# One layer pair on one core: x's first two tiles loaded singly at the head of ScalarE's queue, A and x transposed and the first u taken in the network's waits, loads of SyncE reordered

## What is computed

```python
# layer 0, on x
h = gelu(cond @ W0 + b0); h = gelu(h @ W1 + b1); att = softmax(h @ W2 + b2)
agg_w = einsum('bk,koi->boi', att, weight); agg_b = att @ bias_k
o = einsum('boi,bih->boh', agg_w, x) + agg_b[:, :, None]
logits = o @ Wr.T                      # 4 experts, the best 2, softmax over them
mid = einsum('tf,erf->ter', o, A)
x = x + sum_e gates * einsum('ter,eor->teo', mid, B) * 4
# layer 1, on the new x
o = conv1d(x, weight, 9 taps, 4 groups) + (cond @ c_weight.T)[:, :, None] + bias
h = relu(layernorm(o @ gw1.T + gb1) * gamma + beta); gates = h @ gw2.T + gb2
# 8 experts, best 2, an expert counts only if it was chosen at most 1536 times
x = x + o @ W.T + lora(o, lora_A, lora_B, w) / 16
```

## Time and profile before

| what | us, or as said |
|---|---|
| median of 3 runs | 302.68 |
| lowest and highest | 301.27, 303.99 |
| profiled execution | 302.07 |
| its span, first to last instruction | 300.3 |
| TensorE busy (matmul) | 288.7 |
| VectorE, ScalarE, GpSimd busy | 195.4, 125.3, 95.1 |
| packets of the queue of SyncE, share of the 16 DMA engines' span | 69.1% |
| HBM rate over the span | 175 GB/s |

### The profile page before, as it was taken

One profiled execution on the slowest core, in us unless ns is written; L12 is line 12 of the kernel. 1 busy time (PEld: TensorE's weight loads), 2 busy tenths in 40 slices (PEclk: granted clock), 3 DMA queues, 4 the chain that ended last, 5 costly groups with the idle time before them and its releaser, 6 DMA issues.

```text
span 300.3 us, 6135 instructions
## 1 busy us (share of the span) xinstructions
PE 288.7 (96%) x1982; PEld 236.5 (79%) x1982; DVE 195.4 (65%) x506; ACT 125.3 (42%) x263; POOL 95.1 (32%) x124
## 2 busy tenths in 40 slices
...
GB/s 142 186 339 143 154 252 233 212 213 75 220 185 210 87 218 211 178 93 181 228 189 104 161 224 207 104 154 204 129 104 163 187 206 6 0 2 188 320 331 280
DMA packets 74400, 52.75 MB, mean 176 GB/s; under 512 B 44405, under 2 KB 61477, under 8 KB 74377
## 3 DMA queue, kind: packets, MB, share of 16 engines
q1 hardware_dynamic: 72936, 51.37, 69.1%
...
...
HBM read 35.67 MB, written 16.78 MB: 175 GB/s over the span
## 4 chain that ended last, share of the span: by engine, by line
PE 54%; DMA 14%; SPq 12%; DVE 8%; issue 5%; ACT 4%; POOL 1%; DVEq 0%; ACTq 0%
PE ps_g L1139 10%; PE ps_d L1139 9%; DMA xg<-x1d 8%; PE ps_c L1277 7%; DMA x1d<-xq 7%; PE ps_a L1100 5%; PE ps_t L1293 3%; SPq L353 3%; PE ps_a L1089 3%; SPq L356 2%; ACT xq L632 2%; PE ps_d L1318 2%; PE ps_d L1319 2%; PE ps_d L1500 1%; PE ps_d L1505 1%
## 5 line engine op out<-in xcount | busy, mean ns | idle before, releaser
L512 POOL TENSOR_TENSOR o1l<-o,o1h 128x512 fp32r<-128x512 f32 x30 | 39.4, 1313 | 150.2 <-ACT o L644 150.2
L1139 PE MATMUL ps_d<-wt_hi,o1h 128*128 128x336 f32 (+1 forms) x120 | 41.1, 342 | 0.3 <-DVE y_all L961 0.3
L1139 PE MATMUL ps_d<-wt_hi,o1l 128*128 128x336 f32 (+1 forms) x120 | 38.7, 323 | 0.0
L1139 PE MATMUL ps_d<-wt_lo,o1h 128*128 128x336 f32 (+1 forms) x120 | 38.6, 322 | 0.0
L1277 PE MATMUL ps_c<-xg,cw 96*32 96x512 f32 x256 | 34.1, 604 | 3.1 <-DMA xg<-x1d 3.1
L955 DVE TENSOR_TENSOR oT<-ps_c,biasT 128x512 f32<-128x512 f32 x32 | 21.9, 686 | 22.8 <-PE ps_c L1277 21.9
L1139 PE MATMUL ps_g<-wt_hi,o1h 128*128 128x336 f32 x112 | 35.6, 318 | 0.6 <-ACT tmp_all L659 0.4
L1139 PE MATMUL ps_g<-wt_hi,o1l 128*128 128x336 f32 x112 | 35.5, 317 | 0.0
L1139 PE MATMUL ps_g<-wt_lo,o1h 128*128 128x336 f32 x112 | 35.4, 316 | 0.0
L632 ACT ACTIVATE xq<-y_all 128x512 f32 (+1 forms) x29 | 31.9, 1152 | 7.3 <-DMA x1d<-xq 4.1
L1100 PEld LDWEIGHTS ps_a<-pm,xT 128*128 128x128 f32 x256 | 30.2, 192 | 1.4 <-issue 0.8
...
## 6 DMA issues: line engine op xcount, KB each, us to landing
xg<-x1d SPq DMA_DIRECT2D x64, 254.0 KB, 5.1
...
xs<-in_x_dram SPq DMA_DIRECT2D x6, 1024.0 KB, 6.2
...
y_all<-in_x_dram ACTq DMA_DIRECT2D x2, 512.0 KB, 5.2
y_all<-in_x_dram SPq DMA_DIRECT2D x1, 1024.0 KB, 5.7
```

The source lines that it names most:

```text
L512: pool.tensor_tensor(lo, o1[t % 2][:, :, :], hi.bitcast(fp32), ALU.subtract).then_inc(s_o1l, 1)
L1139: last = T.matmul(bank[:, 0:columns], a[:, Q - 1 - q, :], w[:, q, first:first + columns], start=(q == 0 and n == 0), stop=(q == Q - 1 and ...
```

## The change

- **Loads of x[0].** On ScalarE's queue x[0] came as two halves of 512 KB, fourth and sixth. Now its first tile is the second load, its second tile the fourth, and the last two tiles the fifth. b2 and fside move from there to SyncE's queue.
- **SyncE's loads.** A and Wr (aw) are issued ahead of the four loads of the mixing weights; b2 ahead of them, the context weights and fside behind. The load of x[3] leaves the set-up: it is issued in step 1, ahead of gather(1, 1). Layer 1's A is one load of 1024 runs of 256 B, where it was eight of 512 runs of 64 B each, ahead of the taps; ga is stored as blocks of 16 for that, and three instructions read or write it by blocks.
- **TensorE's head.** A is transposed behind t1(0, 0), ahead of W2's product; t1 and the products of u (`u_first`, into ps_d[1]) are placed one tile at a time; the transposes of B move behind the last of them; the context's transpose and product move back; four `keep_busy` of one are dropped, and two of one become two.
- **B.** ScalarE copies the transposed B twice (b_plain, b_hi), VectorE takes b_lo from the copy behind gates0(0). The bias's transpose moves behind t1(1, 1). delta(0, 0) waits for b_lo.
- The ones are set by VectorE first; GpSimd clears the taps later.

```diff
-        ga = sb("ga", [P, Q, GC])
+        ga = sb("ga", [P, GC // R1, Q, R1])
...
             sp.dma_start(w1n, w1).then_inc(s_ld["w1"], 16)
-            sp.dma_start(ctxn, ctxw).then_inc(s_ld["ctx"], 16)
             sp.dma_start(w2n, w2).then_inc(s_ld["w2"], 16)
+            sp.dma_start(b2b, b2.partition_broadcast(P)).then_inc(s_ld["b2"], 16)
+            sp.dma_start(aw[0:ER0], ffa.rearrange("e r h -> (e r) h")).then_inc(s_ld["aw"], 16)
+            sp.dma_start(aw[ER0:UC], ffr).then_inc(s_ld["aw"], 16)
             sp.wait_ge(s_wk0, 1)
             for j in range(4):
                 sp.dma_start(wk[C * j:C * j + K0],
                              mixw.rearrange("k (o j) i a -> j k o (i a)", j=4)[j])\
                   .then_inc(s_ld["mixw"], 16)
-            sp.dma_start(aw[0:ER0], ffa.rearrange("e r h -> (e r) h")).then_inc(s_ld["aw"], 16)
-            sp.dma_start(aw[ER0:UC], ffr).then_inc(s_ld["aw"], 16)
+            sp.dma_start(ctxn, ctxw).then_inc(s_ld["ctx"], 16)
+            sp.dma_start(fsb, fside.partition_broadcast(P)).then_inc(s_ld["side"], 16)
             sp.dma_start(mbn, row(mixb, 1, BT)).then_inc(s_ld["mixb"], 16)
             for e in range(E0):
...
-            for i in range(2):
-                sp.dma_start(xs[i][:, :, :], x_v[2 + i]).then_inc(s_x[i], 16)
+            sp.dma_start(xs[0][:, :, :], x_v[2]).then_inc(s_x[0], 16)
+            sp.dma_start(ga[:, GB:, :, :].rearrange("p e q r -> p e (q r)"),
+                         lora_a.rearrange("e (m q) r -> m e (q r)", q=Q)).then_inc(s_ld["lora_a"], 16)
             sp.wait_ge(s_zero, 1)
             for i in range(Q):
                 sp.dma_start(taps[i:C:Q, :, 7 - i:7 - i + TAPS],
                              convw.rearrange("o c k -> c o k")).then_inc(s_ld["conv"], 16)
-            for e in range(E1):
-                sp.dma_start(ga[:, :, G1 + e * R1:G1 + (e + 1) * R1],
-                             lora_a[e].rearrange("(m q) r -> m q r", q=Q)).then_inc(s_ld["lora_a"], 16)
...
-                if has(s, 2) and not at_step(s, 0) and not at_step(s, 1):
+                if has(s, 2) and not at_step(s, 0):
...
             act.dma_start(b0c, b0.rearrange("(p a) -> p a", a=1)).then_inc(s_ld["b0"], 16)
+            act.dma_start(xs_early[0][:, 0, :], x_v[0][:, 0, :]).then_inc(s_xf[0], 16)
             act.dma_start(b1c, b1.rearrange("(p a) -> p a", a=1)).then_inc(s_ld["b1"], 16)
-            act.dma_start(b2b, b2.partition_broadcast(P)).then_inc(s_ld["b2"], 16)
-            act.dma_start(xs_early[0][:, 0:NT // 2, :], x_v[0][:, 0:NT // 2, :]).then_inc(s_xf, 16)
-            act.dma_start(fsb, fside.partition_broadcast(P)).then_inc(s_ld["side"], 16)
+            act.dma_start(xs_early[0][:, 1, :], x_v[0][:, 1, :]).then_inc(s_xf[1], 16)
             act.dma_start(xs_early[0][:, NT // 2:NT, :], x_v[0][:, NT // 2:NT, :]).then_inc(s_xh, 16)
...
+                bank = ps_d[1] if at_step(u, 0) else ps_a[0]
+                nc.scalar.activation(u_sb[:, :, :].rearrange("p t c -> p (t c)"), bank[:, 0:NT * UC],
...
+            x_transposed(0, (0,))
             act.wait_ge(s_attd, 1)
             nc.scalar.activation(atte, att, ACT.Exp).then_inc(s_atte, 1)
-            x_transposed(0)
+            x_transposed(0, (1, 2, 3))
             u_out(0)
-            act.wait_ge(s_sp["bias"], 1)
-            nc.scalar.activation(biasT[:, :], ps_t[:, 0:NB], ACT.Copy).then_inc(s_ss["bias"], 1)
+            act.wait_ge(s_sp["b"], 1)
+            nc.scalar.activation(b_plain.rearrange("p c m -> p (c m)"), ps_t[:, :], ACT.Copy).then_inc(s_ss["b_plain"], 1)
+            nc.scalar.activation(b_hi[:, :].rearrange("p (m c) -> p c m", c=HC),
+                                 ps_t[:, :].rearrange("p (c m) -> p c m", c=HC), ACT.Copy).then_inc(s_ss["b_hi"], 1)
...
+            V.memset(ones[:, :], 1.0).then_inc(s_ones, 1)
             V.memset(wk, 0.0)
             V.memset(attw, 0.0).then_inc(s_wk0, 1)
...
+            dve.wait_ge(s_ss["b_hi"], 1)
+            dve.wait_ge(s_ss["b_plain"], 1)
+            V.tensor_tensor(b_lo[:, :].rearrange("p (m c) -> p c m", c=HC), b_plain,
+                            b_hi[:, :].bitcast(fp32).rearrange("p (m c) -> p c m", c=HC),
+                            ALU.subtract).then_inc(s_ss["b"], 1)
...
+            def u_first(tiles):
+
+                for t in tiles:
+                    pe.wait_ge(s_xt, t + 1)
+                    for c in range(HC):
+                        last = T.matmul(ps_d[1][:, t * UC:(t + 1) * UC], xT[:, t, c, :], pm[:, c, :],
+                                        start=(c == 0), stop=(c == HC - 1))
+                if tiles[-1] == NT - 1:
+                    last.then_inc(s_up, 1)
+
+            pe.wait_ge(s_ones, 1)
             keep_busy(2)
             pe.wait_ge(s_const, 1)
             pe.wait_ge(s_ld["cond"], 16)
             T.transpose(ps_c[:, 0:P], condn, idp).then_inc(s_sp["condT"], 1)
-
-            keep_busy(1)
+            keep_busy(2)
             pe.wait_ge(s_ld["w0"], 16)
             pe.wait_ge(s_ss["condT"], 1)
             T.matmul(ps_t[:, 0:P], w0n, condT, start=True, stop=True).then_inc(s_sp["h1"], 1)
-            keep_busy(1)
-            pe.wait_ge(s_ld["ctx"], 16)
-            T.transpose(ps_g[:, 0:C], ctxn, ident[0:C, 0:C]).then_inc(s_sp["ctxT"], 1)
+            keep_busy(2)
             pe.wait_ge(s_ld["w1"], 16)
             pe.wait_ge(s_ss["h1"], 1)
             T.matmul(ps_t[:, 0:P], w1n, h1, start=True, stop=True).then_inc(s_sp["h2"], 1)
             keep_busy(1)
-            pe.wait_ge(s_ss["ctxT"], 1)
-            T.matmul(ps_g[:, 0:C], condT, ctxT, start=True, stop=True).then_inc(s_sp["ctx"], 1)
-            keep_busy(1)
+            pe.wait_ge(s_xf[0], 16)
+            t1(0, xs_early[0], 0)
+            pe.wait_ge(s_ld["aw"], 32)
+            for c in range(HC):
+                last = T.transpose(ps_c[:, c * UC:(c + 1) * UC], aw[:, c * P:(c + 1) * P], ident[0:UC, 0:UC])
+            last.then_inc(s_sp["pm"], 1)
             pe.wait_ge(s_ld["w2"], 16)
             pe.wait_ge(s_ss["h2"], 1)
             T.matmul(ps_t[:, 0:K0], h2, w2n, start=True, stop=True).then_inc(s_sp["att"], 1)
-            keep_busy(1)
-            pe.wait_ge(s_xf, 16)
-            t1(0, xs_early[0], 0)
+            pe.wait_ge(s_xf[1], 16)
             t1(0, xs_early[0], 1)
-            keep_busy(1)
+            pe.wait_ge(s_ss["pm"], 1)
+            u_first((0,))
+            pe.wait_ge(s_xh, 16)
+            t1(0, xs_early[0], 2)
             pe.wait_ge(s_ss["att"], 1)
             T.transpose(ps_v[:, 0:P], attw.rearrange("p j k -> p (j k)"), idp).then_inc(s_sp["attT"], 1)
-            pe.wait_ge(s_xh, 16)
-            pe.wait_ge(s_xt, 1)
-            t1(0, xs_early[0], 2)
-            pe.wait_ge(s_ld["aw"], 32)
-            for c in range(HC):
-                last = T.transpose(ps_t[:, c * UC:(c + 1) * UC], aw[:, c * P:(c + 1) * P], ident[0:UC, 0:UC])
-            last.then_inc(s_sp["pm"], 1)
-            pe.wait_ge(s_xt, 2)
+            u_first((1,))
             t1(0, xs_early[0], 3)
-            pe.wait_ge(s_ss["pm"], 1)
-            u_products(0, (0,))
-            pe.wait_ge(s_bn, 1)
-            for c in range(HC):
-                last = T.transpose(ps_t[:, c * P:(c + 1) * P], bn2[:, c, :, :].rearrange("p d e -> p (d e)"), idp)
-            last.then_inc(s_sp["b"], 1)
-            u_products(0, (1,))
+            pe.wait_ge(s_ld["ctx"], 16)
+            T.transpose(ps_g[:, 0:C], ctxn, ident[0:C, 0:C]).then_inc(s_sp["ctxT"], 1)
+            u_first((2,))
...
-            u_products(0, (2, 3))
-            pe.wait_ge(s_bd, 1)
-            keep_busy(1)
+            u_first((3,))
+            pe.wait_ge(s_ss["ctxT"], 1)
+            T.matmul(ps_g[:, 0:C], condT, ctxT, start=True, stop=True).then_inc(s_sp["ctx"], 1)
+            pe.wait_ge(s_bn, 1)
+            for c in range(HC):
+                last = T.transpose(ps_t[:, c * P:(c + 1) * P], bn2[:, c, :, :].rearrange("p d e -> p (d e)"), idp)
+            last.then_inc(s_sp["b"], 1)
             pe.wait_ge(s_mbsb, 1)
             pe.wait_ge(s_ss["rs"], 1)
             mix(0)
...
             pe.wait_ge(s_ss["ctx"], 1)
+            pe.wait_ge(s_ss["b_hi"], 1)
+            pe.wait_ge(s_ss["b_plain"], 1)
+            T.transpose(ps_t[:, 0:NB], bex, idp).then_inc(s_sp["bias"], 1)
...
+                    pe.wait_ge(s_ss["b"], 1)
                     delta(0, 0)
...
```

59 lines of the change are left out of this document (28 added, 31 removed).

## The result

| what | before | after |
|---|---|---|
| median on the same chip, us | 303.34 (4 executions, 301.27 to 305.29) | 311.94 (4 executions, 308.17 to 315.26) |
| profiled execution, us | 302.07 | 308.17 |
| its span, us | 300.3 | 306.4 |
| TensorE busy, us | 288.7 | 291.1 |
| start of conv(0, 0), conv(1, 0) | 39.95, 59.08 | 37.80, 56.87 |

The change makes the kernel slower: ratio 1.025, 95% interval 1.018 to 1.033. It was forecast at 301.0, with 0.04 for slower. The ratios here leave out executions that the clock disturbed more than others, while medians, lowest and highest hold all of them.

The account below looks back on a forecast made before the run. TensorE, busy 288.7 of 300.3 us, was taken as the bound. From the profiled 302.07, - 0.5 (head) - 2.2 (gather waits) + 1.3 (x[3]) gave 300.7; with 0.3 for the median, 301.0 us, range 298.7 to 303.4.

Parts of the forecast that it names:

- Step 1: TensorE's head up to the first mix: A and Wr land at 8.1, mix(0) at 18.1, 1.0 us early, bounds 0.2 and 2.0.
- the round robin: The skill's page: DMA engines alternate between queues packet by packet, so aw needn't wait for all of x, mix(0) at 17.1.
- Step 2: From the mix to the first delta: gate weights land at 22.7, their transposes and gm_transposed(0) gain 0.5 us.
- Step 3: SyncE's queue: set-up issues end near 26, first write at 28.3 not 31.96, the gap of 1.97 ahead of conv(0, 0) closes.
- Step 4: Behind conv(0, 0): 0.5 us returns as a wait for VectorE; waits of 0.45 and 0.42 close; gain in all 2.7.
- g: The gain at the gate weights' transposes and gm_transposed(0), taken as 0.5 us, bounds 0 and 1.1.
- Step 5: Load of x[3] ahead of gather(1, 1) in step 1 of the loop: conv(1, 1) waits 1.3 us, bounds 0 and 3.7.
- the sum of 1.7: First estimate of conv(1, 1)'s wait: gather lands at 60.3 plus 3.1 for x[3], 63.4, and TensorE wants it at 61.65.
- the loop's row: Step 2 of the loop: gather landed 9.8 us behind x's load; the same in step 1 gives 62.3, a wait of 0.7.
- what lies behind step 1 repeats as before: Claim that the loop after its step 1 keeps its times, since TensorE bounds it; no loss was put there.
- E: Rival: x[3]'s load ahead of gather(1, 1) costs the whole 3.7 us, time 303.4, chance 0.09.
- D: Rival: SyncE's queue stays shut until x[2] is in, first write as late as before, 305.2 us, chance 0.06.

## Why the prediction was wrong

- **Step 1, mis-sized.** mix(0) came at 18.80, a gain of 0.3, not 1.0. A and Wr landed 0.9 later than the 8.1 that I took, and the value that I named as the bound (as late as 9, gain 0.2) is what happened. The reason given, small loads behind the large one of ScalarE's queue, fits, but no run took the large one away; and the round robin did not bring them early.
- **Step 2, mis-sized.** The gate weights landed at 23.07, where I had 22.7, and their transposes ran at 23.11, a gain of 0.1 against 0.5. With little gained before, TensorE hardly waited for them.
- **Step 3, right.** The queue free at 26.1 (26), the first write at 28.76 (28.3), conv(0, 0) at 37.80 without a gap (37.5). I gave its cause as the megabyte and the seven issues together. Each is nearly enough alone: the one load brings the first write to 29.00, the megabyte's move to 29.88, and with either TensorE doesn't wait ahead of conv(0, 0).
- **Step 4, right.** The wait for VectorE was 0.30 (0.5), and the waits ahead of conv(0, 1) and conv(1, 0) closed. The lead at conv(1, 0) was 2.2 (2.7); 0.4 of the missing 0.5 is g, which was 0.1.
- **Step 5, the step that failed.** It said a wait of 1.3 with a bound of 3.7. It was 3.97. TensorE was there at 62.2 and not 61.65. The data landed at 66.2 and not at 63.0, 3.2 late, and three terms make that up. The chain ahead was taken as 3.8 us earlier; the last part of gather(1, 1) was issued at 55.68 against 57.95, 2.3 earlier (1.5). Some 0.5 of that is the lead that steps 1 and 2 missed and 0.5 the issue of x[3] itself; the rest is open. The megabyte was taken as 3.1 us, its bytes at the full rate; it made the gather 4.4 us longer, 10.5 instead of 6.1 (1.3). And I had moved 0.4 from the sum of 1.7 towards the loop's row. My bound took transfers of one queue as served in order, and so closed above with what was ahead. The run with gather(1, 2) held back shows that what comes behind counts too: 1.6 of the 4.4.
- **What no step had.** The clock. The prediction took it as 1.00 throughout, as in the windows before, where the wait of 1.97 had left it there. The wait of 4.0 made it fall, and that cost 2.5 us. Then the load of x[4] made conv(2, 1) wait 1.68 where it was 0.21, another 1.5, and conv(4, 1) waited 0.65. For "what lies behind step 1 repeats as before" I had no row: the spare time of the loop's gathers belonged to a TensorE that came later.
- **The sum.** 302.07 - 2.2 in the fill. Then conv(1, 1) is 1.84 late and no longer 2.21 early: 4.05 more. The clock 2.5, conv(2, 1) 1.5. That is 307.9; the profiled execution took 308.17. The median, 311.94, is higher still, since two of the four executions had a mean clock of 0.96. No step had that, and its cause stays open beyond the count that ties it to the rewritten head.
- **Rivals.** E (x[3] costs the whole 3.7) was the nearest, at 0.09 and 303.4. It had the wait but not what follows from it. D's condition never came: the queue was free at 26.
